# Twelve chunks of a depthwise conv made tap by tap on VectorE, nine TensorE rounds in place of twelve, and a recurrence staged by DMAs

## The reference, cut to what matters

```
x = x + L0(_gn(x))      # bidirectional LSTM over the 64 rows, then a linear map
x = x + L1(_gn(x))      # see below

def L1(x):
    out_standard = conv2d(x, conv_w, conv_b, padding=1)                 # 3x3
    offset_x = offset_branch(x, offx_...)
    offset_y = offset_branch(x, offy_...)
    out_x = dsc_axis(x, offset_x, dscx_w, 'x')    # 9 samples at x + offset, then a sum over channels
    out_y = dsc_axis(x, offset_y, dscy_w, 'y')
    out = conv2d(concat([out_standard, out_x, out_y]), fus_w, None, padding=0)
    return relu(batchnorm(out, fus_bn_g, fus_bn_b))

def offset_branch(x, dw_w, dw_b, bn_g, bn_b, pw_w, pw_b):
    h = conv2d(x, dw_w, dw_b, padding=1, groups=x.shape[1])             # depthwise 3x3
    h = relu(batchnorm(h, bn_g, bn_b))                                  # statistics over images and pixels
    return conv2d(h, pw_w, pw_b, padding=0)
```

## Time and profile before

| what | value |
|---|---|
| median of three runs | 836.1 us (835.29 to 838.27) |
| the profiled execution | 835.34 us, of which 833.4 us span |
| TensorE matmul busy | 728.8 us (87%) |
| VectorE busy | 611.9 us (73%) |
| ScalarE busy | 492.3 us (59%) |
| GpSimd busy | 254.2 us (31%) |
| recurrence | about 33.9 to 199.4 us |
| conv rounds | 229.8 to 342.2 us |
| batch norm between conv and offsets | 342.2 to 353.6 us |
| offsets | 353.6 to 402.4 us |
| sampling loop | 402.4 to 811.6 us |

### The profile page before, as it was taken

How to read it: one execution, slowest core, us unless ns; L and a number is a source line. 1 busy time by engine, 2 the same in 40 slices (tenths; PEclk the granted TensorE clock), 3 DMA queues, 4 the chain that set the end, 5 groups by cost and what they waited for, 6 DMA issues and landing times.

```text
span 833.4 us, 61037 instructions
## 1 busy us (share of the span) xinstructions
PE 728.8 (87%) x27570; PEld 591.5 (71%) x27570; DVE 611.9 (73%) x1126; ACT 492.3 (59%) x1008; POOL 254.2 (31%) x272
## 2 busy tenths in 40 slices
PE   0799999989599999587779999999999999999980
PEld 0455555556268999433569999999989999999970
DVE  5466666665803322578769999999999999999985
ACT  0444444442423332366658878888778788888864
POOL 2122222220000000000235454444465665656631
PEclk9999999999889999789999999999999999999995
DMA  6200000000000000000000000000000000000005
GB/s 241 91 3 1 0 0 0 0 2 1 4 4 4 4 4 4 4 1 1 3 4 0 0 0 0 0 0 0 0 0 0 0 0 0 0 0 0 0 2 201
DMA packets 4062, 12.03 MB, mean 14 GB/s; under 512 B 879, under 2 KB 1275, under 8 KB 3972
## 3 DMA queue, kind: packets, MB, share of 16 engines
q1 hardware_dynamic: 1716, 4.88, 1.6%
q10 hardware_dynamic: 1714, 4.20, 1.4%
q0 software_dynamic: 576, 2.10, 0.6%
HBM read 6.99 MB, written 4.19 MB: 13 GB/s over the span
## 4 chain that ended last, share of the span: by engine, by line
PE 67%; DVE 18%; ACT 8%; issue 4%; DMA 1%; POOL 1%; DVEq 0%; ACTq 0%; POOLq 0%
PE psum L1024 17%; PE psum L953 17%; PE psum L900 13%; PE psum L979 8%; PE psum L971 5%; DVE wide L610 5%; DVE wide L613 4%; ACT wide L425 4%; ACT wide L421 3%; PE psum L923 2%; DVE offs L698 2%; DMA xs<-in_x_dram 1%; DVE stats L645 1%; DVE wide L777 1%; DVE xs L654 1%
## 5 line engine op out<-in xcount | busy, mean ns | idle before, releaser
L511 ACT ACTIVATE wide<-psum 128x512 f32<-128x512 f32 x576 | 301.3, 600 | 13.1 <-PE psum L953 6.2
L953 PE MATMUL psum<-wide,sels 125*32 125x256 bf16 x4608 | 231.1, 274 | 2.6 <-issue 2.0
L1024 PE MATMUL psum<-wide 128*32 128x64 f32 x8192 | 193.8, 219 | 3.1 <-issue 3.1
L722 DVE TENSOR_SCALAR wide<-wide 128x1024 f32<-128x1024 f32 x256 | 180.3, 725 | 1.2 <-ACT wide L511 1.1
L1024 PEld LDWEIGHTS psum<-wide 128*32 128x32 f32 x8192 | 168.4, 109 | 4.7 <-issue 3.6
L729 DVE COPY wide<-psum 128x1024 f32<-128x1024 f32 x128 | 156.0, 1219 | 2.0
L361 POOL COPY wide<-offs 125x256 bf16 (+1 forms) x64 | 28.9, 451 | 386.8 <-DVE offs L698 212.9
L353 POOL TENSOR_SCALAR wide<-wide 128x512 f32<-128x512 f32 x64 | 136.5, 2133 | 7.2 <-ACT wide L511 7.2
L900 PE MATMUL psum<-img,offs 32*32 32x512 f32 x3456 | 112.4, 610 | 5.8 <-ACT img L453 5.8
L979 PE MATMUL psum<-wc,wide 32*64 32x128 f32 x4096 | 112.7, 283 | 1.3 <-issue 1.3
L818 PEld LDWEIGHTS psum<-wide 128*64 128x64 f32 x2048 | 70.3, 137 | 61.0 <-DVE wide L621 60.0
(11 more groups left out here) (101 smaller groups left out, 772.1 us busy)
## 6 DMA issues: line engine op xcount, KB each, us to landing
xs<-in_x_dram ACTq DMA_DIRECT2D x4, 512.0 KB, 8.5
xs<-in_x_dram SPq DMA_DIRECT2D x4, 512.0 KB, 8.0
out_dram<-wide SPq DMA_DIRECT2D x4, 512.0 KB, 4.0
out_dram<-wide POOLq DMA_DIRECT2D x4, 512.0 KB, 4.8
offs<-in_cw_dram ACTq DMA_DIRECT2D x1, 576.0 KB
sels<-in_sel_dram ACTq DMA_DIRECT2D x1, 562.5 KB
wide<-in_dsc_dram ACTq DMA_DIRECT2D x1, 288.0 KB
offs<-in_dwd_dram ACTq DMA_DIRECT2D x1, 288.0 KB
```

What stands on the lines that cost most here:

```text
L511: nc.scalar.activation(hat_tile(par, i), use_bank(par, hat_use(i)).rearrange("p (q n) -> p q n", q=2), ACT.Abs).then_inc(d_read, 1)
L722: nc.vector.tensor_scalar(v, v, 1.0, 1.0, ALU.min, ALU.subtract).then_inc(v_ready, 1)
L953: last = mm(bank[c, e * SL:(e + 1) * SL], sels[:, k, c], oc[0:NROW, par, :], start=(e == 0), stop=(e == 1))
L1024: last = mm(ps[O_BANK][C * q:C * q + C, cols], w, v, start=(group == 0), stop=(group == GROUPS - 1))
```

## The change: what it does

1. **Conv rounds.** Twelve of the sixteen chunks of `h_x` are made on VectorE. They form three blocks of four chunks (`ON_DVE` = 0, 4, 8), each one tile of 128 x 2048 elements. A block takes nine operations: a first tap with the bias, and eight operations that multiply a shifted view of `pad` by the tap's weight and add the block itself (`scalar_tensor_tensor`). The first tap of the second and third block is made by ScalarE ahead of its evacuations. TensorE has 36 chunk jobs left, in nine rounds: in the first eight, two of the y branch, one conv, and in turn one of the x branch or another conv; the ninth holds four conv jobs. ScalarE now evacuates all three kinds, and the places are chosen so that a round's pieces are whole or halves; in the ninth round two jobs are cut into four. The weights of the taps come with `vecs`, which is 23 columns wide instead of 14.
2. **Batch norm.** The statistics of both branches are complete after the eighth round. TensorE issues the mean's small matmul two taps ahead of the end of the ninth round and the variance's behind it. ScalarE evacuates the ninth round around the norm: two jobs ahead of `relu_y_round`, one behind it, and one behind the first evacuation of the offsets. The wait of the first offset matmuls for the whole conv is split by bank.
3. **Recurrence.** `stage_x` and `store_h` are DMAs on SyncE's queue: two of 128 x 512 elements per group for the inputs, and one of 64 x 512 and four of 64 x 128 for the states. SyncE's list per group is: wait for `x_used`, stage the group after next, wait for both halves' states, store them. `xst` is laid out so that the DMA copies in order, and TensorE reads the backward direction with a negative step. GpSimd does nothing in the recurrence.

The diff, cut to its core:

```diff
-        PLACES = {0: 0, 2: 1, 1: 2}
-        TURN = (0, 2, 1)
-        ...
+        ON_DVE = (0, 4, 8)
+        DW_CHUNKS = 4
+        def conv_rounds():
+            conv, hy, hx = iter(range(NCH)), iter(range(NCH)), iter(range(DW_CHUNKS * len(ON_DVE), NCH))
+            rounds = []
+            for m in range(8):
+                rounds.append([(0, 0, next(conv)), (1, 2, next(hy)),
+                               (2, 0, next(conv)) if m % 2 else (2, 1, next(hx)), (3, 2, next(hy))])
+            rounds.append([(i, 0, next(conv)) for i in (0, 2, 1, 3)])
+            return rounds
...
 SyncE:
+            def stage_x(group):
+                for d, f0 in ((0, group * GROUP), (1, S - (group + 1) * GROUP)):
+                    sp.dma_start(xst[:, group % 2, d], xg[:, :, f0:f0 + GROUP, :]).then_inc(xst_ready[group % 2], 16)
+            def store_h(group):
+                f0, tile = group * GROUP, hst[:, group % 2 * GROUP:(group % 2 + 1) * GROUP]
+                for b in range(2):
+                    sp.wait_ge(h_ready[b], (group + 1) * GROUP + 1)
+                sp.dma_start(hall[0:DQ, f0:f0 + GROUP].rearrange("p f b t -> p f (b t)"), tile[0:DQ]).then_inc(h_stored[group % 2], 16)
+                for j in range(GROUP):
+                    sp.dma_start(hall[DQ:P, S - 1 - f0 - j].rearrange("p b t -> p (b t)"), tile[DQ:P, j]).then_inc(h_stored[group % 2], 16)
+            sp.wait_ge(xg_ready, 2)
+            stage_x(1)
+            for group in range(NG - 1):
+                if group + 2 < NG:
+                    sp.wait_ge(x_used, group + 1)
+                    stage_x(group + 2)
+                store_h(group)
...
 ScalarE:
+            for n in ON_DVE[1:]:
+                src, to = dw_block(n)
+                nc.scalar.activation(to, src(0), ACT.Identity, bias=vecs[:, V_DWB:V_DWB + 1], scale=dw_weight(0)
+                                     ).then_inc(dw_first, 1)
...
+            for m in range(CONV_ONLY):
+                for k in range(4):
+                    evacuate(m, k)
             norm_sqrt(BN, 2)
+            for k in range(2):
+                evacuate(CONV_ONLY, k)
...
             relu_y_round(0)
+            evacuate(CONV_ONLY, 2)
...
+                        if rd == 0 and done is part1[0] and n == 0:
+                            evacuate(CONV_ONLY, 3)
...
 VectorE:
+            for k, n in enumerate(ON_DVE):
+                src, to = dw_block(n)
+                if k == 0:
+                    dve.wait_ge(pad_ready[0], 1)
+                    step(nc.vector.tensor_scalar(to, src(0), dw_weight(0), vecs[:, V_DWB:V_DWB + 1], ALU.mult, ALU.add))
+                else:
+                    dve.wait_ge(pad_ready[n // (NCH // 2)], 1)
+                    dve.wait_ge(dw_first, k)
+                for t in range(1, K):
+                    step(nc.vector.scalar_tensor_tensor(to, src(t), dw_weight(t), to, ALU.mult, ALU.add))
+                for c in range(DW_CHUNKS):
+                    dw_stats(1, n + c)
+                for m in ((0, 1), (2, 3, 4), (5, 6, 7))[k]:
+                    last = round_stats(m)
...
 TensorE:
+                    if m == CONV_ONLY and t == K - 2:
+                        norm_mean(BN, 2)
...
-            norm_mm(BN, 2)
-            pe.wait_ge(conv_ev, NCH)
+            norm_var(BN, 2)
...
+                    if rd == 0 and n != 1:
+                        pe.wait_ge(conv_ev, NCH - 2 + max(n - 1, 0))
```

More of the change, by code:

```diff
@@ L163, in build @@
         h_ready = [sem(f"h_ready{b}") for b in range(2)]
[L164 to L165 removed]
+        xst_ready = [sem(f"xst_ready{par}") for par in range(2)]; x_used = sem("x_used")
+        h_stored = [sem(f"h_stored{par}") for par in range(2)]; h_last = sem("h_last")
         pool_turn = sem("pool_turn")
@@ L211, in build, with conv_bank, dw_block, src @@
         NORM_BANK = 7
-        PLACES = {0: 0, 2: 1, 1: 2}
-        TURN = (0, 2, 1)
-        CONV_ROUNDS, made = [], [0, 0, 0]
-        for m in range(3 * NCH // 4):
-            kinds = (0, 2, 1, TURN[m % 3])
-            CONV_ROUNDS.append([])
-            for j in kinds:
-                CONV_ROUNDS[m].append((j, made[j]))
-                made[j] += 1
-        X_PLACE = {n: i for jobs in CONV_ROUNDS for i, (j, n) in enumerate(jobs) if j == 1}
-        def conv_bank(m, i):
-            return ps[4 * (m % 2) + i]
+        ON_DVE = (0, 4, 8)
[8 more added lines that the diff above has]
+            return rounds
+        CONV_ROUNDS = conv_rounds()
+        CONV_ONLY = len(CONV_ROUNDS) - 1
+        JOB_NO, X_PLACE, Y_PLACE = {}, {n: 0 for n in range(DW_CHUNKS * len(ON_DVE))}, 1
+        for jobs in CONV_ROUNDS:
+            for i, j, n in jobs:
+                JOB_NO[j, n] = sum(1 for key in JOB_NO if key[0] == j) + 1
+                if j == 1:
+                    X_PLACE[n] = i
+        def conv_bank(m, k):
+            return ps[4 * (m % 2) + k]
+        def dw_block(n):
+            b, r0, rows = n // (NCH // 2), n % (NCH // 2) * ROWS, DW_CHUNKS * ROWS
+            def src(t):
+                return pad[:, b, r0 + t // 3:r0 + t // 3 + rows, t % 3:t % 3 + S]
+            return src, hxv[:, b, r0:r0 + rows, :]
+        def dw_weight(t):
+            return vecs[:, V_DWW + t:V_DWW + t + 1]
         ROUNDS = 4
@@ L295, in _ @@
             nc.gpsimd.memset(hst, 0.0).then_inc(zeroed, 1)
-            nc.gpsimd.nop().then_inc(h_stored, 2)
-            def stage_x(rows, rows_b, par):
-                nc.gpsimd.tensor_copy(xst[:, par, 0].rearrange("p f (b t) -> p f b t", b=2),
-                                      xg[:, :, rows, :].rearrange("p b f t -> p f b t"))
-                nc.gpsimd.tensor_copy(xst[:, par, 1, ::-1].rearrange("p f (b t) -> p f b t", b=2),
-                                      xg[:, :, rows_b, :].rearrange("p b f t -> p f b t")).then_inc(xst_ready, 1)
-            def store_h(rows, rows_b, par, count, stores, staged):
-                for b in range(2):
-                    pool.wait_ge(h_ready[b], count)
-                pool.wait_ge(xst_ready, staged)
-                pool.sem_inc(pool_turn, 1)
-                tile = hst[:, par * GROUP:(par + 1) * GROUP]
-                nc.gpsimd.tensor_copy(hall[0:DQ, rows].rearrange("p f b t -> p f (b t)"), tile[0:DQ]).then_inc(hf_stored, 1)
-                pool.wait_ge(hf_stored, stores)
-                pool.sem_inc(pool_turn, 1)
-                nc.gpsimd.tensor_copy(hall[DQ:P, rows_b].rearrange("p f b t -> p f (b t)"), tile[DQ:P, ::-1]
-                                      ).then_inc(h_stored, 1)
+            for par in range(2):
+                nc.gpsimd.nop().then_inc(h_stored[par], STORE)
             def halve(w, by):
@@ new lines, in _, with evacuate @@
+            for b in range(2):
+                act.wait_ge(pad_ready[b], 1)
+            for n in ON_DVE[1:]:
+                src, to = dw_block(n)
+                nc.scalar.activation(to, src(0), ACT.Identity, bias=vecs[:, V_DWB:V_DWB + 1], scale=dw_weight(0)
+                                     ).then_inc(dw_first, 1)
+            def evacuate(m, k):
+                i, j, n = CONV_ROUNDS[m][k]
+                made_by, done = ((conv_mm, conv_ev), (hx_mm, hx_ev), (hy_mm, hy_ev))[j]
+                bias = cbias if j == 0 else vecs[:, V_DWB + j - 1:V_DWB + j]
+                act.wait_ge(made_by, JOB_NO[j, n])
+                turns = (i, 0, (i - Y_PLACE) % Q)[j]
+                for own, at in {0: ((slice(0, P), slice(0, P)),),
+                                2: ((slice(0, S), slice(S, P)), (slice(S, P), slice(0, S)))}.get(
+                                    turns, [(slice(C * q, C * q + C), slice(C * ((q + turns) % Q), C * ((q + turns) % Q) + C))
+                                            for q in range(Q)]):
+                    src = conv_bank(m, k)[at, :]
+                    if j == 2:
+                        to, src = hy_chunk(n, own), src.rearrange("p (h w) -> p w h", h=ROWS)
+                    else:
+                        to = (acc, h_x)[j][own, n * CH:(n + 1) * CH]
+                    last = nc.scalar.activation(to, src, ACT.Identity, bias=bias[at, 0:1])
+                last.then_inc(done, 1)
@@ L888, in _ @@
                 if m >= 2:
-                    for j, n in CONV_ROUNDS[m - 2]:
-                        read[j] = n + 1
+                    for i, j, n in CONV_ROUNDS[m - 2]:
+                        read[j] = JOB_NO[j, n]
                     pe.wait_ge(conv_ev, read[0])
```

123 lines of the change are left out of this document (45 added, 78 removed).

## The result

The changed kernel takes 798.2 us in the median of four runs (797.04 to 799.62) against 836.7 for the kernel before (835.29 to 838.27). The ratio is 0.954, with a 95% interval of 0.9516 to 0.9564. The forecast was 791.0 with a range of 785 to 805: the direction and the range held, the point was 7 us too low. By the profiled executions the change brought 35.7 us (835.3 to 799.6) where the sum had 44.7, so 9.0 us are to be explained.

The account below looks back on a forecast made before the run. TensorE was taken to bound the conv rounds, and a chain through TensorE, ScalarE and VectorE the recurrence. 835.3 - 14.0 - 33.2 + 2.5 = 790.6 us, given as 791.0 against 836.1, range 785 to 805.

Parts of the forecast that it names:

- Term 1: Recurrence: without GpSimd's copies slowing VectorE, 120 half steps at 1.15 us take 138.0 instead of 152.61 us; 14.0 us taken.
- Hidden even at 7 us: Recurrence start: first staging by DMA, issued at about 25 us, wanted at 32.5, so it costs nothing even at 7 us.
- The margin of the stages in the loop: Recurrence: input stages land 7.3 us behind a group's end, wanted at 9.2, so 1.9 us to spare.
- Rival B: Recurrence: DMA writes slow VectorE as GpSimd's copies did, or stages land late; term 1 is lost, 805 us; chance 0.09.
- Rival C: Recurrence: staging lands late in every group, slower than before from 9.5 us per landing, up to 865 us; chance 0.05.
- Terms 2 and 3: Conv and batch norm: three 9.10 us rounds less, norm beside the ninth round; together the offsets start 33.2 us earlier.
- Rival A: Conv: dearer taps make VectorE the bound; 822 us at 3.8 us per tap, 803 at 3.0; chance 0.08.
- Term 4: First offset part: the fourth bank waits for ScalarE's late pieces of the ninth round, a loss of 2.5 us.

Follow-up runs that it names:

- conv-only version: The kernel before with only the conv, batch norm and evacuation changes, GpSimd still copying in the recurrence: 808.2 us against 836.2, ratio 0.9677.

## Why the prediction was right, and where the 9 us are

The mechanisms of all four terms were right. **Term 1 is the step that was mis-sized**: 14.0 taken, 10.65 measured (10.5 of it in the 120 half steps that it was worked out for). These take 142.12 us, 4.1 over 138.0.
- 1.7 us of them are eight half steps of 1.35 to 1.41 us, seven of them 16 apart and one among the first steps. They stand in before and after alike, so they aren't the copies'; I had charged all but 0.6 us of the excess of before to the copies. Pricing only the slowed half steps in the timeline of before, seven of 2.04 us, six pairs of 1.64 and 1.58 and a last pair of 1.64 and 1.30, gives 7 x 0.89 + 6 x 0.92 + 0.64 = 12.4 us.
- 1.3 us are the first half step, 2.48 us long (1.43 in before). "Hidden even at 7 us" failed: this stage took 9.1 us to land, and TensorE waited. It was issued while the weights were still being loaded (the DMA engines were busy 0.62 of the time from 25 to 34 us, 0.27 in the recurrence). Staging by VectorE gave 1.4 us of the 120 half steps back, which shows that this transfer was the cost; that the loads held it up is only argued from the shares and from the landing of 2.6 us in the loop. Landings of 4.7 to 11.6 us among loads stood in the earlier trace rows; I used them for the groups in the loop, where they don't apply, and not here.
- 1.1 us are fifteen half steps of 1.21 to 1.23 us, fourteen of them at the places of former slow ones. Their cause wasn't sought.

The mechanism stood: without copies the operation stays at 225 ns, and with half of them back most of the cost returns. The margin of the stages in the loop came out by luck: the seven issues took 4.4 us instead of 2.9 and the landing 2.6 instead of 4.4, so the two misses cancel (7.0 us behind the group's end, predicted 7.3). Rival B had said that DMAs might slow VectorE in their place. 0.27 of the DMA engines' time was in use, and the maximum of 128 operations is 227 ns: refuted. The Trainium skill (SBUF — State Buffer, "SBUF: two separate sides") holds that DMAs and engines use separate sides, and that GpSimd and VectorE exclude each other on a shared port pair for the whole instruction; the trace agrees with the first half (a maximum of 227 ns beside the DMAs) and with the second (the operations that end 0.07 to 0.15 us behind the copy). Rival C needed landings of 9.5 us in every group; their median was 2.6, and no stage after the first was waited for. The Trainium skill (DMA: Bandwidth & Descriptors, "Anatomy of one DMA") gave an estimate of 2.6 us for a stage, which is the measured median, though not the 9.1 of the first one.

**Unforeseen, +3.3 us: the clock around the linear map.** Here nothing in the instructions changed. The four matmuls of 1.98 us took 3.78 while the granted clock was at 0.50, and half of those 6.6 us is the 3.3 that is missing. The fall comes with either part of the change alone, and with the copies half restored (198 to 202 us), so it isn't the DMAs, nor VectorE's taps. TensorE was busy without a gap ahead of it (11.00 of 11.00 us in the conv-only version), and just so in before, where no fall follows. Its cause stays open. What the profiles show: the seven falls at the linear map cost 1.7 us (four of them) or 3.2 to 3.3 us (three) from the last cell operation to the mean's copy, the four profiles of before have none, and nothing in the rows of before announced it.

**Terms 2 and 3, 33.2 predicted, 33.78 measured** (32.8 by the second profile of the changed kernel). The rounds ran at 9.12 us (9.10 taken). A tap took 2.351 us (2.28 worked out from the slope of two smaller shapes), 3% more, which used up 1.7 us of VectorE's time over 24 taps and none of the end's. The norm's small matmuls took 0.38 us instead of about 0.6, and the first offset matmul follows the variance's by 5.2 us instead of 5.5. Rival A came at four taps more, so the rival was close: VectorE's margin is about one tap and a half in 24.

**Term 4, 2.5 predicted, 2.54 measured**, and given back by moving the four pieces.

**Later stages.** The first cell operation comes between 33.10 and 33.93 us in four profiles of before and between 32.85 and 34.69 in the changed ones, so +0.76 is within what executions differ by. From the loop to the end before took 431.0 to 432.6 us, so +0.9 is as well. The later offset parts (+1.5) ran in part at a lower clock:

```profile
340.90:353.70 12.80, 10.41 (x87) 3.63 (x88) 10.00 (x8) 8.46 (x8) 0.00 (x0) 0.77 0.00 1
```

The same part took 11.5 us at a mean of 0.93 in before. These parts alternate short matmul bursts with waits. From the second part to the loop the second profile of the changed kernel took 35.3 us instead of 36.5, and before 34.7 to 34.9.

So of the 9.0 us missing, 3.35 are term 1, 3.3 the clock at the linear map, 1.5 the later offset parts (put down to the clock, not shown by an experiment), and the rest is within what executions differ by. The point of the forecast also holds a slip: 790.6 + 0.8 is 791.4, not 791.0.

## What to carry to other kernels

In a dependent chain, charge a slowed operation only with its excess over its neighbours, not the chain's mean over its cleanest step: part of the excess is the loop's own. A transfer that is hidden in the steady state needs its own estimate at the start, where it shares the DMA engines with the loads. When work goes from TensorE to VectorE, count the margin in operations; in the one profile of an overrun here, it cost itself and, behind the wait, 1.7 us at the lower clock.

## What was unexpected of the hardware

- TensorE's granted clock fell to 0.50 while TensorE was busy without a gap, for 3 to 7 us, once in each of ten profiles of changed kernels and in none of four of the kernel before; in the same program it was once at 36 us, behind a wait of 2.46 us, and once at 189 us.
- DMAs from SBUF to SBUF landed after 2.6 us (256 KB), 2.2 (128 KB) and 1.9 (32 KB) in the median, and took SyncE's queue 0.63, 0.50 and 0.60 us each to issue, not the 0.42 of the loads.
- Every lengthened `scalar_tensor_tensor` on VectorE, 74 in two profiles, had started under a GpSimd copy and ended 0.07 to 0.15 us behind the copy's end. Two copies back to back cost the chain 1.2 of the 1.7 us per 16 half steps that four copies cost.
- Matmuls that nobody reads, ahead of the conv, brought its first evacuation from 10.1 to 8.8 us behind its start.
